# Cross-attention on one core: statistics of the first sequences from another layout of x, loads reordered, and the inverse root by log and exp

## The reference, cut to what matters

```python
N, C, S, S2, H = 16, 64, 256, 256, 8           # 16 sequences, 8 heads of 64 channels
mu  = mean(x, axis=(1, 2)); var = var(x, axis=(1, 2))          # one pair for each sequence
xn  = (x - mu) * rsqrt(var + 1e-5) * gamma[None, :, None] + beta[None, :, None]
q   = Wq @ xn + bq;   k, v = split(Wkv @ context + bkv)        # by head
att = softmax(q.T @ k / 8)                                     # 256 x 256 for each head
out = x + Wo @ concat_heads(att @ v) + bo
```

## Time and profile before

| | us |
|---|---|
| median of 3 runs | 231.10 |
| lowest, highest | 230.66, 232.79 |
| the profiled execution: span from first to last instruction | 228.2 |
| what lies around the span (median less span) | 2.9 |

### The profile page before, as it was taken

How to read it: one execution, slowest core, us unless ns; L and a number is a source line. 1 busy time by engine, 2 the same in 40 slices (tenths; PEclk the granted TensorE clock), 3 DMA queues, 4 the chain that set the end, 5 groups by cost and what they waited for, 6 DMA issues and landing times.

```text
span 228.2 us, 7194 instructions
## 1 busy us (share of the span) xinstructions
PE 208.6 (91%) x2511; PEld 179.9 (79%) x2511; DVE 199.3 (87%) x589; ACT 181.1 (79%) x371; POOL 160.3 (70%) x157
## 2 busy tenths in 40 slices
PE   6968878799999999999999998999999999999872
PEld 6857757588888798889888887888888888887761
DVE  3589987879898999899999999999999998989765
ACT  2374586787889988898889888989897979888880
POOL 5135185777987877789788887789686869776460
PEclk9975897999999999999999999999999999999998
DMA  5964137480767566566665665656657656442000
GB/s 134 261 272 93 27 82 174 107 184 14 164 141 160 131 153 142 132 141 151 140 153 122 160 151 121 151 127 154 142 127 166 149 133 143 93 94 62 13 3 23
DMA packets 31090, 29.04 MB, mean 127 GB/s; under 512 B 4240, under 2 KB 29840, under 8 KB 31056
## 3 DMA queue, kind: packets, MB, share of 16 engines
q1 hardware_dynamic: 30224, 28.07, 52.4%
q10 hardware_dynamic: 832, 0.53, 1.0%
HBM read 3.80 MB, written 1.05 MB: 21 GB/s over the span
## 4 chain that ended last, share of the span: by engine, by line
PE 41%; POOL 20%; issue 13%; ACT 11%; DVE 11%; ACTq 2%; POOLq 0%; DVEq 0%
POOL p_lo L773 19%; PE ps_sc L522 6%; PE ps_max L546 6%; PE ps_sc L523 5%; PE ps_z L479 4%; ACT p_full L678 4%; DVE neg_max L894 4%; ACT p_hi L675 3%; PE ps_z L481 3%; PE ps_z L480 3%; PE ps_z L414 3%; PE ps_m L589 2%; PE ps_t L497 2%; PE ps_m L590 2%; DVE z_sum L910 2%
## 5 line engine op out<-in xcount | busy, mean ns | idle before, releaser
L773 POOL TENSOR_TENSOR p_lo<-p_full,p_hi 128x512 f16<-128x512 f32 x122 | 139.9, 1163 | 42.3 <-ACT p_full L678 41.2
L675 ACT ACTIVATE p_hi<-ps_sc 128x512 f16<-128x512 f32 x128 | 77.9, 608 | 18.3 <-PE ps_sc L523 15.9
L894 DVE TENSOR_REDUCE neg_max<-ps_max 128x2 f32<-128x512 f32 x128 | 85.9, 677 | 6.9 <-PE ps_max L546 6.8
L678 ACT ACTIVATE p_full<-ps_sc 128x512 f32<-128x512 f32 x128 | 78.7, 615 | 0.0
L522 PE MATMUL ps_sc<-t_a,c_seq 128*128 128x256 f32 x256 | 71.2, 300 | 3.5 <-issue 2.6
L523 PE MATMUL ps_sc<-t_b,c_seq 65*128 65x256 f32 x256 | 67.3, 284 | 0.0
L479 PEld LDWEIGHTS ps_z<-u_hi,p_hi 128*128 128x128 f16 x512 | 46.4, 97 | 12.8 <-issue 8.2
L479 PE MATMUL ps_z<-u_hi,p_hi 128*128 128x65 f16 x512 | 53.0, 195 | 2.2 <-DVE p_lo L930 1.9
L522 PEld LDWEIGHTS ps_sc<-t_a,c_seq 128*128 128x128 f32 x256 | 49.2, 192 | 5.9 <-issue 4.6
L480 PE MATMUL ps_z<-u_lo,p_hi 128*128 128x64 f16 x512 | 52.8, 193 | 0.0
L481 PE MATMUL ps_z<-u_hi,p_lo 128*128 128x65 f16 x512 | 52.7, 194 | 0.0
(11 more groups left out here) (108 smaller groups left out, 233.9 us busy)
## 6 DMA issues: line engine op xcount, KB each, us to landing
t_a<-t_a SPq DMA_DIRECT2D x90, 128.0 KB, 2.4
t_b<-t_b SPq DMA_DIRECT2D x30, 128.0 KB, 2.5
x_seq<-x_hi SPq DMA_DIRECT2D x15, 128.0 KB, 2.4
c_pad<-c_hi SPq DMA_DIRECT2D x30, 64.0 KB, 2.1
c_seq<-c_hi SPq DMA_DIRECT2D x15, 128.0 KB, 2.4
x_res<-x_tiles SPq DMA_DIRECT2D x4, 256.0 KB, 6.7
out<-x_res SPq DMA_DIRECT2D x16, 64.0 KB, 2.0
x_seq<-x_lo SPq DMA_DIRECT2D x15, 64.0 KB, 2.1
```

Source lines behind the costliest of these rows:

```text
L675: nc.scalar.activation(p_hi[:, buf, :, :].rearrange("p t s -> p (t s)"), scores, ACT.Exp).then_inc(act_phi, 1)
L678: nc.scalar.activation(p_full[:, head % 2, :], scores, ACT.Exp).then_inc(act_p, 1)
L773: nc.gpsimd.tensor_tensor(p_lo[:, buf, :, :].rearrange("p t s -> p (t s)"), p_full[:, head % 2, :], p_hi[:, buf, :, :].rearrange("p t s -> ...
L894: nc.vector.tensor_reduce(to, ps_max[:, unit % 2, :].rearrange("p (t s) -> p t s", t=KT), X, ALU.max, negate=True).then_inc(dve_max, 1)
```

## The change

- `bn_stats` reads columns of `x_raw` (two sequences side by side, so `mean_w` becomes two blocks of 64 by 64), in two groups: columns 0 and 1 (the first four sequences) in the opening, columns 2 to 7 in steps 2 and 3 of DVE. Group 1 has its mean on PE in step 4, deviations on DVE and variance on PE in step 5, its root on ACT in step 6, and its factors on POOL at the head of step 7 (seven small instructions).
- The loads are reordered: columns 0 and 1 of `x_raw` first, `x_res` last. The first load of `x_raw` has two columns.
- The square root and its table go; ACT takes ln and then exp with scale -0.5, with one table set named ahead.
- DVE normalises columns 0 and 1, POOL column 2 in step 9.
- The maxima of the context (`c_tops`) move from steps -8, -8, -7 to the ends of steps -4, -3, -2, the transposes of `tops` from -6 to -2, `top` from -5 to -1, the bound on PE from -4 to -1, `u_scale` from -1 to 0. `t_b` of the early turns moves one step later, behind the maxima. ACT's copy of b moves from before the steps to step -6.
- The second piece of staging of x on SP goes from step -1 to step 1. The two `keep_warm` matmuls before the steps go.

```diff
-T_LO_FIRST = (0, 0, 0, 1, 2, 3, 4, 4, 5, 6, 6, 6, ...
+T_LO_FIRST = (0, 0, 0, 0, 1, 2, 3, 4, 5, 6, 6, 6, ...
-X_STAGE_FIRST = (-8, -1)
+X_STAGE_FIRST = (-8, 1)
-C_TOP_AT = (-8, -8, -7)
-TOP_AT, UNSCALE_AT, B_LOW_AT = -5, -1, 1
-TOPS_AT, BOUND_AT = -6, -4
-POOL_XN_AT = (-6, -2)
+C_TOP_AT = (-4, -3, -2)
+TOP_AT, UNSCALE_AT, B_LOW_AT = -1, 0, 1
+B_COPY_AT, TOPS_AT, BOUND_AT = -6, -2, -1
+POOL_XN_AT = (9,)
+STATS_AT, MEAN_AT, DEV_AT, VAR_AT, ROOT_AT, NORM_AT = (2, 3), 4, 5, 5, 6, 7
-X_LOADS = ((0, 1), (1, 4), (4, 8))
+X_LOADS = ((0, 2), (2, 4), (4, 8))
+X_GROUPS = ((0, 2), (2, 8))
...
+            load_x(0)
+            load_c(0)
+            sp.dma_start(w_sb[0:C, 0:W_BO], w_in[:, 0:W_BO]).then_inc(dma_w, 16)
+            load_c(1)
+            load_x(1)
+            load_c(2)
+            load_x(2)
             for c in range(N // CHUNK):
                 sp.dma_start(x_res[:, chunk(c), :], x_tiles_in[:, chunk(c), :]).then_inc(dma_xt[c], 16)
...
+            def mean(g):
+                first, end = X_GROUPS[g]
+                pe.wait_ge(dve_stats, end)
+                for a in range(2):
+                    last = mm(stat_bank(g)[:, first:end], mean_w[:], parts(g, 1)[:, :, a], start=(a == 0), stop=(a == 1))
+                last.then_inc(pe_mean, 1)
+
+            def variance(g):
+                first, end = X_GROUPS[g]
+                pe.wait_ge(dve_spread, g + 1)
+                pe.wait_ge(dve_q, g + 1)
+                moving = [t[:, first:end, a] for t in (spread, dev2) for a in range(2)]
+                for i, columns in enumerate(moving):
+                    last = mm(stat_bank(g)[:, N + first:N + end], mean_w[:], columns, start=(i == 0), stop=(i == len(moving) - 1))
+                last.then_inc(pe_var, 1)
...
             keep_warm(WARM_MEAN)
+            mean(0)
             pe.wait_ge(dma_qk, 16 * 2)
             products_a(0)
+            variance(0)
             products_a(1)
...
             products_b()
-            keep_warm(WARM_T)
...
+                if n * H + h == MEAN_AT:
+                    pe.wait_ge(dve_tlo, PAIRS)
+                    mean(1)
+                if n * H + h == VAR_AT:
+                    variance(1)
...
+            nc.scalar.preload_act_table_set("natural_log_exp_and_others")
+            def inverse_root(g):
+                first, end = X_GROUPS[g]
+                act.wait_ge(dve_var, g + 1)
+                nc.scalar.activation(log_var[:, first:end], var[:, first:end], ACT.Ln).then_inc(act_log, 1)
+                act.wait_ge(act_log, g + 1)
+                nc.scalar.activation(y0[:, first:end], log_var[:, first:end], ACT.Exp, scale=-0.5).then_inc(act_root, 1)
...
+            statistics(0, FIRST_XN)
+            spreads(0)
+            deviations(0)
+            variances(0)
+            dve.wait_ge(act_root, 1)
...
+            nc.vector.tensor_scalar(xn[:, 0, :], x_raw[:, 0, :], xn_scale[:, 0:1], xn_shift[:, 0:1], ALU.mult, ALU.add).then_inc(dve_xn, 1)
             a_low(0)
...
+                for part, when in enumerate(STATS_AT):
+                    if n * H + h == when:
+                        per = (N // 2 - FIRST_XN) // len(STATS_AT)
+                        statistics(FIRST_XN + part * per, FIRST_XN + (part + 1) * per)
+                        if part == len(STATS_AT) - 1:
+                            spreads(1)
+                if n * H + h == DEV_AT:
+                    deviations(1)
+                if n * H + h == ROOT_AT:
+                    variances(1)
```

More of the change, by code:

```diff
@@ L629, in _ @@
                                  scale=xn_scale[0:C, 0:1]).then_inc(act_x0, 1)
[L630 removed]
+            xn_ready(act, 0)
             nc.scalar.activation(x_hi[:, 0, :], xn[:, 0, :], ACT.Copy).then_inc(act_xhi, 1)
[L632 to L635 removed]
             def transpose_out(m, part):
@@ L688, in step @@
                     transpose_out(*e)
+                if n * H + h == B_COPY_AT:
+                    act.wait_ge(dve_btop, 1)
+                    for k in range(2):
+                        nc.scalar.activation(b_sb[k * C:(k + 1) * C], ps_sc[0:C, 1, :], ACT.Copy).then_inc(act_b, 1)
+                if n * H + h == ROOT_AT:
+                    inverse_root(1)
                 if n * H + h == B_HIGH_AT:
@@ L810, in _ @@
-            parts = stats[:].rearrange("p n (a k) -> p n a k", a=2)
-            chain(nc.vector.tensor_tensor(dev[:], parts[:, :, :, 1], mu2, ALU.subtract))
-            chain(nc.vector.tensor_tensor(dev2[:], dev[:], dev[:], ALU.mult))
-            nc.vector.scalar_tensor_tensor(out=dev2[:], in0=parts[:, :, :, 2], scalar=2.0 / P, in1=dev2[:], op0=ALU.mult,
-                                           op1=ALU.add).then_inc(dve_q, 1)
-            for k in range(2):
-                rows = slice(k * C, (k + 1) * C)
-                nc.vector.tensor_scalar_add(mu_2[rows], mu[rows].rearrange("p (j k) -> p k j", k=2)[:, k], 0.0)
@@ L818, in _ @@
-            dve.wait_ge(pe_var, 1)
-            for k in range(2):
-                rows = slice(k * C, (k + 1) * C)
-                spread = ps_m[rows, 64:64 + 2 * N].rearrange("p (j k a) -> p k j a", k=2, a=2)
-                last = nc.vector.tensor_reduce(var[rows], spread[:, k], X, ALU.add)
-            chain(last)
-            nc.vector.tensor_scalar_add(var[:], var[:], EPS).then_inc(dve_var, 1)
-            a_low(0)
-            dve.wait_ge(act_root, 1)
-            chain(nc.vector.reciprocal(y0[:], root[:]))
@@ L835, in _, with statistics, spreads @@
-            nc.vector.tensor_scalar(xn_shift[:], xn_shift[:], -1.0, w_sb[:, W_BETA:W_BETA + 1], ALU.mult, ALU.add).then_inc(dve_scale, 1)
+            def statistics(first, end):
+                for j in range(first, end):
+                    loaded(dve, X_LOADS, dma_x, j)
+                    nc.vector.bn_stats(stats[:, j, :], x_raw[:, j, :]).then_inc(dve_stats, 1)
+            def spreads(g):
+                first, end = X_GROUPS[g]
+                dve.wait_ge(dve_stats, end)
+                nc.vector.tensor_scalar(spread[:, first:end, :], parts(g, 2), 1.0 / P, 0.0, ALU.mult, ALU.add).then_inc(dve_spread, 1)
@@ new lines, in _ @@
+            chain(last)
+            for j in cols:
+                last = nc.vector.tensor_scalar(y2[:, j:j + 1], y1[:, j:j + 1], -3.0, y0[:, j:j + 1], ALU.add, ALU.mult)
+            chain(last)
+            dve.wait_ge(dma_w_tail, 32)
+            first = slice(0, FIRST_XN)
+            nc.vector.tensor_scalar(xn_scale[:, first], y2[:, first], w_sb[:, W_GAMMA:W_GAMMA + 1], -0.5, ALU.mult, ALU.mult)
+            chain(nc.vector.tensor_scalar(neg_scale[:, first], y2[:, first], w_sb[:, W_GAMMA:W_GAMMA + 1], 0.5, ALU.mult, ALU.mult))
```

191 lines of the change are left out of this document (108 added, 83 removed).

## The result

| | before | after |
|---|---|---|
| median of 5 runs each, on one chip | 230.66 | 240.50 |
| lowest, highest | 228.95, 232.79 | 238.96, 240.85 |
| profiled execution, span | 228.2 | 236.2 |

The ratio is 1.048, 95% interval 1.040 to 1.055: slower by some 10 us where 1.2 were forecast, and outside the range.

A forecast was written before the change was run, and what follows sets the result against it. DVE was taken to bound the kernel up to 28 us, PE after the ninth head. That head 1.2 us later made the span 228.2 + 1.2 = 229.4; with 2.9 around it, 232.3 us, range 229.2 to 234.8.

The forecast's parts named there:

- The factors: Opening: factors of x for group 0 ready at 13.2 us against 15.76, so 2.55 us earlier.
- The table: ACT's second table load, 1.28 us, lay beside DVE's Newton step; taking it away gives 0 by itself.
- the ping-pong rival: ln and exp given two table sets, adding 1.28 us twice: 234.9 us in all; chance 0.06.
- The sign: Whole kernel: slower, with the ninth head and the span 1.2 us later than before.
- head 0 would wait anyway: Opening: PE's wait for `tops` ahead of turn 4, a maximum and turn 5 costs head 0 nothing.
- DVE's sum: DVE's queued work from the factors to head 0's scores, ending at 27.1 us.
- 0.9 us earlier: First scores, those of head 0, at 27.1 us where they were at 28.00 before.
- the new chain of group 1: Step 5: deviations 0.75, variance 1.0, queued PE work 0.8 us; transposes of sequence 1 at 42.6 instead of 40.36.
- PE's own work up to the ninth head: From the transposes of sequence 1 to the ninth head: 3.9 us less overlap, so 46.3.
- DVE's idle time: From 28 to 40.3 us, some 2.3 us of gaps take all 2.2 us of group 1's statistics.
- low clock rival: PE meets its dense work at half clock after the new waits, losing 1.7 us: 234.0 us; chance 0.21.
- the first turn: Opening: first turn of t at 14.7 us against 17.17, so 2.4 us earlier.

The follow-up runs named there:

- e8: Changed kernel with group 1 later, bound on u and order of `t_b` back, POOL kept aside in the opening; 233.09 us beside 229.61, ratio 1.018.
- e9: e8 with POOL's factors spread over steps 12 to 15, root, variance and `x_res` addition earlier, columns 2 and 3 later; 230.65 us beside 228.96, ratio 1.014.
- b1: Kernel before the change, with only the late bound on u and its order of `t_b`; 232.71 us beside 228.96, ratio 1.024.
- e2: Changed kernel with group 1 left out, later columns of x taking the factors of column 0; 232.44 us beside 230.23, ratio 1.017.
- e10: Changed kernel with group 1 left out and the bound on u and order of `t_b` back; 228.05 us beside 229.40, ratio 0.999.
- e6: Changed kernel with ten extra small matmuls on PE ahead of the transposes of `tops`; 239.23 us beside 229.61, ratio 1.042.
- e4: Changed kernel with the bound on u back in its old steps, order of `t_b` as changed; 237.57 us beside 230.23, ratio 1.041.
- e7: Changed kernel with group 1 later, nothing left out: stats in steps 4 and 6, root 12, factors 13; 234.26 us beside 229.61, ratio 1.022.
- e3: Changed kernel with nine extra small matmuls on PE ahead of the mean and variance of group 1; 238.47 us beside 229.61, ratio 1.039.
- e5: Changed kernel with POOL made to wait for DVE at three places; 239.17 us beside 230.23, ratio 1.049.

## Why the prediction was wrong

Right: PE bound from the ninth head on, so a delay there arrives in full (8.1 us at head 8, 8.0 at the end). A lead didn't: those of e8 and e9 were lost behind it. The factors, forecast at 13.2, were there at 12.95, in part by luck. The warming matmuls took 5.46 us and not 6.61, so the mean started at 6.95 and not at 8.25; but then PE had another wait that the prediction hadn't:
```profile
8.35 1.15 PE L446 MATMUL ps_max<-wk_sb,p_hi 64*128 64x128 f32 x8 [0.89 <-DMA wk_sb<-wk]
```
Of 1.3 us gained this left 0.4, the variance at 9.43 for 9.8. The table cost nothing either way: one load at 3.29, none later, so the ping-pong rival is out. The mechanism for group 1 was named: PE holds in step 5, with head 6 and the transposes behind it. The sign was right. Its size was not, by a factor of seven or so.

**The step that failed first: "head 0 would wait anyway".** The wait of PE for `tops` was seen (5 us) and costed at nothing, since DVE was taken to be last. b1 gives it 3.8 us (1.7 to 3.1%) in the kernel before, and from e2 to e10, where group 1 is out, the ratio goes from 1.017 to 0.999, though with intervals that overlap. DVE's sum was not bad: its last low part for head 0 ended at 27.98 where 27.1 was forecast. But behind `tops` PE had turn 4, a maximum, the bound and turn 5 to do at half clock, 2.7 us from 26.9 to the scores at 29.68. e6, which leaves the wait and lifts the clock, brings the exp of head 0 from 30.77 to 28.94. Of the prediction's "0.9 us earlier" came 1.7 later. The last maximum of sequence 1 ended at 42.76 for 40.0, and the bound is only a part of that: with the bound back (e4) it ends at 41.18, and without group 1, though head 0 is 0.8 us later than in the changed kernel (e2), the transposes behind it start at 41.66.

**The step that failed most: the new chain of group 1.** From the last maximum to the transposes 2.6 us were forecast (40.0 to 42.6); 4.7 were measured. The terms, as forecast and as measured: deviations 0.75, and 1.5 (42.68 to 44.17), of which 0.93 is the collision with `p_lo`; variance 1.0, and 1.7 from its start to head 6, since "1.0" was PE's work at the full clock; head 6, maximum and transposes 0.8, and 1.4, again at half clock. Ahead of the chain, in the 2.8 us by which the last maximum was late, lies a wait of PE of 1.18 us for the stats in step 4: each stats instruction took 0.41 by itself and 0.36 in a row, not 0.33, with maxima and `u_lo` ahead of them. And behind it, on the way on from the transposes, "PE's own work up to the ninth head", 3.9 us as forecast, was 54.04 - 47.45 - 0.80 = 5.8, the first part of it at half clock. Sum of the errors at head 8: 2.8 (last maximum), 2.1 (the chain), and 54.04 - 47.45 = 6.6 for the 4.5 forecast on the way to head 8, 2.1: 7.0 in all, on a forecast of 47.1, which gives 54.1 (54.04 measured).

**DVE's idle time.** The prediction let gaps of 2.3 us take the 2.2 us of statistics. A gap is not a place: the stats stand in a queue. Before, DVE waited there four times, three times for ACT (0.38, 0.46 and 0.74 us, for `b_w` and `u_hi`) and once for PE (0.81). In the changed kernel waits of 1.15 and 0.60 us stand ahead of the first stats, which can't use them, and from 36.04 to 44.17 DVE has no gap. e7 shows the same work at little or no cost to heads 5 to 8 (0.0 to 0.8 us late, with the late bound still in), when it is put where PE has other work and doesn't wait.

**The low clock rival** had the right mechanism and a price of 1.7 us. Its rule was that PE loses half of the slow time if dense. Here it met the dependent work: at 44 to 52 PE was busy at half clock while the others stood nearly still, so each slow matmul delayed all. Still e3 and e6 give the clock only some 0.7 to 3 us at the marks; the waits themselves are the larger part (e2, e7). A rival with the waits of both passes and the half clock together, at 240, wasn't there. The 2.9 us that the sum has around the span were not the launch's (1.8); they cancel, since forecast and median before both have them.

**POOL and DVE.** The prediction took 0.35 and 0.42 for the normalisation and the low part of x; they took 0.79 and 0.96. e5 shows that the difference is POOL's instruction beside them. The Trainium skill, "SBUF — State Buffer", section "SBUF: two separate sides", says that DVE and GpSimd share a pair of ports by an exclusive lock, for an instruction of DVE with two SBUF inputs (against one of GpSimd that reads SBUF) or in a two-port mode, and that the loser blocks for the whole instruction. The traces agree: 1.10 us at 43.07 end with the 1.15 at 43.00. With that the prediction's 14.7 for the first turn would have been 15.7, had the queues been laid beside each other; from factors 0.25 earlier, 15.46 was measured. With the low part of the context (0.94 for 0.42) the collisions are 1.5 us, more than the whole error of DVE's sum. In the time they are worth nothing that e5 could find, but e5 put others in their place.

**What was kept** of the early factors: 1.3 to 2.1 us at head 0 (b1 against the kernels with the changed opening). By themselves (e10) they are 0.9 us there and 1.9 at the end of the span, too little to tell from no change. So even a change without the two mistakes wouldn't have paid measurably, and e9, with everything in it, doesn't: after head 8 it pays for the variance on a PE without gaps, and for ACT's wait for POOL. That these two are the whole loss is read from the marks of one execution; no run takes them away one at a time.
